# A graph convolution with residual and layer norm on one core: column bands of 1024, wider tiles, and transfers issued from two engines

## The chip, the cores and the metric

The kernel runs on one core of one Trainium2 chip. The metric is the device time of one execution in microseconds (us). Engines are called PE (TensorE, the matmul engine), DVE (VectorE), ACT (ScalarE), POOL (GpSimd) and SP (SyncE, which here only issues transfers). PEld is the weight load of PE, which runs beside its matmuls. A name with q behind it (SPq, ACTq) is the queue of transfers that the engine issues.

## The reference

```python
def reference(x, adj, L0_gnn_w):            # x 8192x128, adj 8192x8192, w 128x128, all float32
    A = adj + jnp.eye(8192)
    deg = jnp.sum(A, axis=1)
    d_isqrt = jax.lax.rsqrt(deg)
    A_hat = A * d_isqrt[:, None] * d_isqrt[None, :]
    y = x + jax.nn.elu(jnp.matmul(jnp.matmul(A_hat, x), w))
    return (y - mean(y)) / sqrt(var(y) + 1e-05)      # over the last axis
```

adj is 268 MB and dominates everything. Each of its elements is wanted twice: in a row sum, and in the product with x. Column j of the product needs the scale of row j of x, and so the whole of row j's sum, before it can be multiplied.

## The kernel before

adj is cut into 16 x 16 tiles of 512 rows by 512 columns (1 MB each). SBUF has `SLOTS` = 20 buffers for tiles (`tile0` to `tile19`), the last three of which are used at the end for the rows of the result.

A function `plan()` writes the order of the work out ahead of time. The columns are taken one after the other (`COLUMNS`: 14 single ones and the last two together). Before the products of column t can start, the rows of block t must have been read whole, because they give the scale of x's block t. So plan() alternates: it reads the rest of the rows of block t+1, and multiplies column t. Of a row block, some tiles to the right are kept in SBUF (`KEEP`, 7 or 8) until their column comes. The others are read for their row sum alone (kind `sum_only`) and read once more later (kind `again`). That makes 331 loads of 1 MB: 62 `keep`, 119 `stream` (below the diagonal, read once), 75 `sum_only` and 75 `again`. So 256 tiles are loaded for a product.

A tile for a product is laid out so that DVE's transpose of 32 x 32 blocks turns it: partition quadrant q (32 partitions) holds the columns 128q to 128q+127 of the tile, for 16 groups of 32 rows. Its load is 8 transfers of 128 KB, all issued by SP (L339): 4 quadrants times `PARTS` = 2 halves. Each contiguous piece in memory is 128 floats, 512 bytes. A `sum_only` tile is one transfer of 1 MB (L335) with pieces of 2 KB. SP waits before each load until the slot's last user is done.

Row sums are taken by ACT (L427, one activation with an accumulated sum for each group of 128 columns, or of 512 in a `sum_only` tile) for three tiles of five, and by POOL and DVE for the others: POOL adds halves (L389) and quarters (L393), and DVE reduces the rest (L574). POOL also adds 1 to the diagonal (L379). DVE turns the tile in place (L569). PE multiplies it: 4 matmuls of 512 columns in the source, which the trace shows as 8 MATMUL rows, since a float32 matmul is carried out in two (L502). DVE adds the product from PSUM to `hT` (L648, L646).

When a row block is read, DVE adds its partial sums (`row_base`, `row_sum`, L613), PE spreads them over the partitions (`p_deg`, L489), DVE copies the degree (L630), POOL raises it to -0.5 (L371), and DVE scales x (L637). SP loads x (L347) into a ring of 4.

The end of a row block of the result: PE multiplies `hT` by w (`p_out`, L475), ACT scales and takes relu and exp (L451 to L458), DVE makes the elu (L523), POOL adds x (L410), DVE takes the statistics (L532, L536), POOL the inverse deviation (L399, L403), DVE normalises (L543), and ACT stores (L440).

Each engine's order comes from the times that plan() works out from four costs:

```python
    LOAD, PRODUCT, SUMS, TURN = 2.91, 3.50, 4.2, 5.2
```

## Time and profile before

| | |
|---|---|
| median of 3 runs | 1421.13 us (1414.34 to 1422.74) |
| the profiled execution | 1416.74 us |
| its span, from the first to the last instruction | 1414.6 us |
| busy: PE, DVE, ACT, POOL | 961.3, 884.1, 642.2, 484.1 us |
| moved by DMA | 360.68 MB, mean 255 GB/s |
| mean granted clock of TensorE | 0.865 of full speed |

The busy times are those of single instructions, added up. A matmul's row is longer than its turn on the engine, because consecutive matmuls overlap. The last line is the share of its full clock that TensorE was granted.

### The profile page before, as it was taken

The page shows a single profiled execution, that of the slowest core. Times are in us where ns is not written, and L with a number is a line of the kernel's source. Part 1 is how long each engine was busy: PE and PEld are TensorE (multiplying, and loading weights), DVE is VectorE, ACT ScalarE, POOL GpSimd, SP SyncE. Part 2 cuts the span into 40 slices and gives each one's busy share as a digit, 9 for nine tenths or more (in the row PEclk, how much of TensorE's full clock was granted, in tenths as well). Part 3 has the DMA queues.
Part 4 walks back from the last instruction along what each step waited for, and adds up shares of the span by engine and source line. Part 5 has one row for each costly group of instructions (what it writes and reads, how often), then busy time and mean ns, then how long its engine had stood idle before and what let it go on. Part 6 is the DMA issues. An engine that isn't in the chain of part 4 may idle for free.

```text
span 1414.6 us, 12892 instructions
## 1 busy us (share of the span) xinstructions
PE 961.3 (68%) x2304; PEld 422.5 (30%) x2304; DVE 884.1 (62%) x979; ACT 642.2 (45%) x3713; POOL 484.1 (34%) x358
## 2 busy tenths in 40 slices
PE   0086097087095392956859495959687796899995
PEld 0032043033042141422324142424233342344542
DVE  0175275385364674746758574756657694988995
ACT  4576476456474563754626453333432202002333
POOL 3434434544434444233343333241312214101333
PEclk9999598599598696987979797979897898999998
DMA  9999999999999999999999999999999999999982
GB/s 305 248 259 328 299 246 316 283 240 317 249 244 313 255 304 257 240 287 257 271 237 282 238 271 238 247 243 249 248 238 238 253 240 242 235 205 242 270 200 66
DMA packets 624528, 360.68 MB, mean 255 GB/s; under 512 B 37056, under 2 KB 586048, under 8 KB 624448
## 3 DMA queue, kind: packets, MB, share of 16 engines
q1 hardware_dynamic: 606016, 351.48, 108.2%
q10 hardware_dynamic: 18432, 8.40, 2.6%
q14 instruction: 62, 0.51, 0.1%
q8 instruction: 18, 0.29, 0.1%
HBM read 355.53 MB, written 4.19 MB: 254 GB/s over the span
## 4 chain that ended last, share of the span: by engine, by line
issue 51%; POOL 28%; PE 11%; SPq 6%; DVE 3%; DMA 0%; POOLq 0%; ACT 0%; ACTq 0%; DVEq 0%
POOL halves L389 16%; PE p_prod L502 10%; POOL quarters L393 9%; SPq L339 5%; POOL tile L379 2%; DVE tile L569 2%; PE p_out L475 1%; SPq L335 1%; POOL d L371 1%; DVE hT L648 1%; DMA tile<-in_adj 0%; POOL tile L410 0%; DVE sums L622 0%; POOL rstd L403 0%; SPq L347 0%
## 5 line engine op out<-in xcount | busy, mean ns | idle before, releaser
L502 PE MATMUL p_prod<-tile,xs 128*128 128x512 f32 x2048 | 945.9, 622 | 90.4 <-DVE tile L569 83.7
L427 ACT ACTIVATE tile<-tile 128x128 f32<-128x128 f32 (+1 forms) x1800 | 586.1, 327 | 599.5 <-DMA tile<-in_adj 597.7
L569 DVE STREAM_TRANSPOSE tile<-tile 128x2048 f32<-128x2048 f32 x256 | 586.7, 2296 | 80.2 <-DMA tile<-in_adj 57.6
L502 PEld LDWEIGHTS p_prod<-tile,xs 128*128 128x128 f32 x2048 | 403.8, 200 | 610.0 <-issue 603.8
L389 POOL TENSOR_TENSOR halves<-tile 128x1024 f32<-128x1024 f32 x109 | 256.0, 2348 | 583.6 <-DMA tile<-in_adj 579.2
L427 ACT ACTIVATION_READ_ACCUMULATOR tile<-tile 128x1 f32 x1800 | 336.8, 187 | 0.0
L489 PE MATMUL p_deg<-rsum,same 128*32 128x4 f32 x128 | 4.4, 199 | 345.7 <-DVE rsum L613 340.3
L648 DVE TENSOR_TENSOR hT<-p_prod,hT 128x512 f32<-128x512 f32 x224 | 146.7, 660 | 16.8 <-PE p_prod L502 16.7
L393 POOL TENSOR_TENSOR quarters<-halves 128x512 f32<-128x512 f32 x109 | 137.9, 1265 | 8.6
L574 DVE TENSOR_REDUCE row_part<-quarters 128x16 f32<-128x512 f32 x30 | 20.4, 679 | 147.7 <-POOL quarters L393 147.7
L574 DVE TENSOR_REDUCE col_part<-quarters 128x16 f32<-128x512 f32 x50 | 33.8, 677 | 125.7 <-POOL quarters L393 125.5
L489 PEld LDWEIGHTS p_deg<-rsum,same 128*32 128x32 f32 x128 | 3.1, 131 | 357.3 <-DVE rsum L613 278.4
L574 DVE TENSOR_REDUCE far_part<-quarters 128x4 f32<-128x512 f32 x29 | 19.9, 686 | 116.1 <-POOL quarters L393 116.1
L451 ACT ACTIVATE tile<-p_out,d 128x128 f32<-128x128 f32 x64 | 18.2, 368 | 159.6 <-PE p_out L475 158.8
L379 POOL TENSOR_TENSOR tile<-tile,ident 128x128 f32<-128x128 f32 x64 | 27.2, 457 | 100.7 <-DMA tile<-in_adj 100.7
L371 POOL TENSOR_TENSOR d<-deg,power 128x4 f32<-128x4 f32 x16 | 16.3, 1017 | 104.9 <-DVE deg L630 104.9
L637 DVE TENSOR_SCALAR xs<-xs,d 128x128 f32<-128x128 f32 x64 | 26.2, 472 | 25.2 <-POOL d L371 25.2
L410 POOL TENSOR_TENSOR tile<-tile 128x512 f32<-128x512 f32 x16 | 20.3, 1269 | 55.2 <-DVE tile L523 53.1
L399 POOL TENSOR_SCALAR var_eps<-mv 128x4 f32<-128x4 f32 x16 | 7.8, 488 | 70.2 <-DVE mv L536 70.2
L543 DVE TENSOR_SCALAR tile<-tile,mv,rstd 128x128 f32<-128x128 f32 x64 | 19.4, 366 | 2.7 <-POOL rstd L403 2.7
L475 PEld LDWEIGHTS p_out<-w_sb,hT 128*128 128x128 f32 x128 | 16.7, 191 | 7.3 <-issue 7.2
L403 POOL TENSOR_TENSOR rstd<-var_eps,power 128x4 f32<-128x4 f32 x16 | 16.6, 1037 | 1.3
(28 smaller groups left out, 122.6 us busy)
## 6 DMA issues: line engine op xcount, KB each, us to landing
tile<-in_adj SPq DMA_DIRECT2D x2048, 128.0 KB, 4.0
tile<-in_adj SPq DMA_DIRECT2D x75, 1024.0 KB, 12.8
xs<-in_x SPq DMA_DIRECT2D x64, 64.0 KB, 3.6
tile<-in_x ACTq DMA_DIRECT2D x64, 64.0 KB, 5.0
out_rows<-tile ACTq DMA_DIRECT2D x64, 64.0 KB, 2.5
w_sb<-in_w SPq DMA_DIRECT2D x1, 64.0 KB, 1.9
```

The lines of the kernel that those rows point to most:

```text
L339: sp.dma_start(tiles[slot][quadrant(q), part], adj_v[s, t, q, :, part]).then_inc(loaded[slot], 16)
L371: nc.gpsimd.tensor_tensor(d[:, r], deg[:, :], power[:, :], ALU.pow).then_inc(d_ready, 1)
L379: nc.gpsimd.tensor_tensor(diag[:, b, :, 32 * b:32 * b + 32], diag[:, b, :, 32 * b:32 * b + 32], ident[:, :, :], ALU.add).then_inc(pool_ste ...
L389: nc.gpsimd.tensor_tensor(half, view[:, :, 0:c], view[:, :, c:2 * c], ALU.add).then_inc(pool_halved, 1)
L393: nc.gpsimd.tensor_tensor(quarter, half[:, :, 0:c // 2], half[:, :, c // 2:c], ALU.add)\
L427: ins = nc.scalar.activation(view[:, g], view[:, g], ACT.Copy, accum_out=sum_at(k)[:, g:g + 1])
L475: ins = nc.tensor.matmul(p_out[n % 2][:, b], hT[:, s, b], w_sb[:, :], start=True, stop=True)
L502: ins = nc.tensor.matmul(p_prod[nth % BANKS][:, :].rearrange("f (g i) -> f g i", g=G), xs[:, t % XRING, b], chunks[:, b], start=(t == cols ...
L569: nc.vector.transpose(tiles[slot][:, :, :], tiles[slot][:, :, :]).then_inc(tile_turned, 1)
L574: nc.vector.tensor_reduce(sum_at(arg), of_rows(how, quarters[:, pool_nth[arg] % 2]), AX.X, ALU.add)\
L637: ins = nc.vector.tensor_scalar(xs[:, r % XRING, b], xs[:, r % XRING, b], d[:, r, b:b + 1], None, ALU.mult)
L648: nc.vector.tensor_tensor(rows, product, rows, ALU.add).then_inc(product_added, 1)
```

## The change

adj is now cut into 8 column bands of 1024 columns (`WIDTHS`), and a tile is 256 rows by 1024 columns (still 1 MB; `rows_of(t)` = 256, `chunk(t)` = 256). There are 32 tiles in a band, 256 in all. In a partition quadrant the contiguous piece is now 256 floats, 1 KB.

Tiles are kept by one rule (`kept_units`): a tile on or above the diagonal is kept if at most `KEEP` = 14 are alive at every band from its rows' band to its own. What is not kept is read for its row sum as `natural`: 128 rows by 2048 columns, pieces of 8 KB (or two blocks of 128 rows by 1024 columns where an odd band is left, pieces of 4 KB). It is read again for the product.

A tile for a product is loaded by 4 transfers of 256 KB: quadrants 0 and 1 are issued by SP, quadrants 2 and 3 by ACT, each behind a wait for the slot. On ACT they stand in order between the row sums.

plan() is now a list scheduler. It plays through events (landed, summed, turned, multiplied), with at most 4 loads in flight, and each engine takes the first of its ready operations by rank. Its orders (`order["sp"]`, `["act"]`, `["pool"]`, `["dve"]`, `["pe"]`) are what the engines then execute, with semaphores. ACT or POOL takes a row sum by which of them would end it sooner. The bookkeeping for a degree is simpler: one table `part` for tiles and one `far` for natural loads, two reductions on DVE, and more small matmuls into `p_deg`. x is scaled by one DVE operation a band, and its ring has 3 places of twice the size. A product is 8 matmuls of 256 columns in the source. The rows of the result are loaded and stored by one transfer a step instead of four.

The core of the diff:

```diff
-NB = 16
-B = N // NB
-G = B // 32
-SLOTS = 20
-XRING = 4
-PARTS = 2
-KEEP = [7, 8, 8, 8, 8, 8, 8, 8, 8, 8, 7, 8, 8, 3, 8, 8]
+WIDTHS = [1024] * 8
+UNIT = 128 * 2048
+SLOTS = 20
+LATE = 3
+KEEP = 14
+XRING = 3
+SP_QUADRANTS = (0, 1)
+ACT_QUADRANTS = (2, 3)
...
+def kept_units():
+
+    spans = []
+    for t in range(BANDS):
+        for u in range(N // rows_of(t)):
+            r = band_of_row(u * rows_of(t))
+            if r <= t:
+                spans.append((t, -r, u))
+    alive, kept = [0] * BANDS, set()
+    for t, r, u in sorted(spans):
+        if all(alive[m] < KEEP for m in range(-r, t + 1)):
+            kept.add((t, u))
+            for m in range(-r, t + 1):
+                alive[m] += 1
+    return kept
...
+    def issue():
+
+        nonlocal dma, at_row, at_col, row_todo, col_todo
+        while in_flight[0] < 4:
+            coming = sum(1 for k in range(max(0, len(loads) - 24), len(loads)) if loads[k][0] != "natural"
+                         and loads[k][1] <= at_row - 1 and (loads[k][1], loads[k][2]) not in product_of)
+            usable = SLOTS - LATE if late() else SLOTS
+            slots = [s for s in free if s[1] < usable]
+            if not slots:
+                return
+            from_rows = row_todo and (not col_todo or coming >= 5)
...
             sp.dma_start(w_sb[:, :], w).then_inc(w_loaded, 16)
-            for k, (kind, s, t, slot) in enumerate(loads):
...
-                    for q, g in ((q, g) for pair in ((0, 2), (1, 3)) for g in range(0, G, G // PARTS) for q in pair):
-                        part = slice(g, g + G // PARTS)
-                        sp.dma_start(tiles[slot][quadrant(q), part], adj_v[s, t, q, :, part]).then_inc(loaded[slot], 16)
...
+                k, load = arg, loads[arg]
+                wait_slot_free(sp, k)
+                if load[0] == "natural":
+                    _, r, k0, nk, x0, wide = load
+                    row = STARTS[r] + 128 * k0
+                    source = adj[row:row + 128 * nk, x0:x0 + wide].rearrange("(k p) c -> p k c", p=128)
+                    sp.dma_start(tiles[slot_of[k]][:, 0:nk * wide].rearrange("p (k c) -> p k c", k=nk), source)\
+                      .then_inc(loaded[slot_of[k]], 16)
                 else:
...
+                    for q in SP_QUADRANTS:
+                        sp.dma_start(as_unit(tiles[slot_of[k]][quadrant(q)], t), quadrant_source(t, u, q))\
+                          .then_inc(loaded[slot_of[k]], 16)
...
         @block.scalar
         def _(act):
+            def issue(k):
+
+                _, t, u = loads[k]
+                wait_slot_free(act, k)
+                for q in ACT_QUADRANTS:
+                    act.dma_start(as_unit(tiles[slot_of[k]][quadrant(q)], t), quadrant_source(t, u, q))\
+                       .then_inc(loaded[slot_of[k]], 16)
+
+            def row_sums(k):
+
+                act.wait_ge(loaded[slot_of[k]], arrived[k])
+                view = as_summed(k, tiles[slot_of[k]][:, :])
                 for g in range(view.shape[1]):
                     ins = nc.scalar.activation(view[:, g], view[:, g], ACT.Copy, accum_out=sum_at(k)[:, g:g + 1])
                 ins.then_inc(act_summed, 1)
...
+                    chunks = tiles[slot_of[k]][:, :].rearrange("p (g b i) -> p b g i", b=nb, i=32)
+                    for b in range(nb):
+                        ins = nc.tensor.matmul(p_prod[n % BANKS][:, 0:rows_of(t)].rearrange("f (g i) -> f g i", i=32),
+                                               xs[:, t % XRING, b], chunks[:, b], start=b == 0, stop=b == nb - 1)
+                    ins.then_inc(product_out, 1)
```

## Rows read from the trace of the kernel before

**Rows 1.** The page: busy time of each engine with share, and packets by size.

```profile
PE 961.3 (68%) x2304; PEld 422.5 (30%) x2304; DVE 884.1 (62%) x979; ACT 642.2 (45%) x3713; POOL 484.1 (34%) x358
...
DMA packets 624528, 360.68 MB, mean 255 GB/s; under 512 B 37056, under 2 KB 586048, under 8 KB 624448
```

**Rows 2.** Waits: engine and line, whom it waited for, us in total, times, longest.

```profile
ACT tile L427 <- DMA tile<-in_adj: 597.7, 73, 51.0
POOL halves L389 <- DMA tile<-in_adj: 579.2, 71, 38.0
...
PE p_prod L502 <- DVE tile L569: 83.7, 28, 10.1
```

**Rows 3.** The page's DMA issues: count, KB each, median us from issue to landing.

```profile
tile<-in_adj SPq DMA_DIRECT2D x2048, 128.0 KB, 4.0
tile<-in_adj SPq DMA_DIRECT2D x75, 1024.0 KB, 12.8
```

**Rows 4.** Windows: length, busy us and count by engine, clock, DMA share, GB/s.

```profile
15.00:20.00 5.00, 0.00 (x0) 0.00 (x0) 0.00 (x0) 3.89 (x14) 0.75 (x1) 1.00 1.05 386
...
100.00:105.00 5.00, 5.00 (x13) 2.24 (x12) 3.21 (x4) 2.13 (x15) 4.54 (x3) 1.00 1.22 272
...
130.00:135.00 5.00, 1.58 (x4) 0.38 (x2) 1.22 (x3) 4.68 (x16) 0.00 (x0) 0.96 1.05 387
...
1350.00:1355.00 5.00, 5.00 (x13) 2.22 (x12) 4.97 (x15) 2.62 (x7) 0.80 (x2) 1.00 1.19 301
```

**Rows 5.** Line L339 from 100 to 119 us: its issues, duration in ns, min/median/max.

```profile
L339 SPq DMA_DIRECT2D tile<-in_adj x39: 448/451/481, 99.8 to 118.5; - x39
...
DMA to landing us min/median/max: 3.3/3.6/4.9
```

**Rows 6.** SP's timeline: start, length of the run of issues, line, count.

```profile
119.54 23.54 SPq L335 DMA_DIRECT2D tile<-in_adj  x12
...
1181.62 1.74 SPq L347 DMA_DIRECT2D xs<-in_x  x4
1183.40 178.23 SPq L339 DMA_DIRECT2D tile<-in_adj  x296
```

**Rows 7.** SP's own waits, the longest for a compute engine.

```profile
SPq L339 <- PE p_prod L502: 20.9, 23, 6.6
```

**Rows 8.** Windows of the product stage and of its last part (columns as in Rows 4).

```profile
200.00:300.00 100.00, 52.23 (x118) 22.12 (x117) 54.57 (x51) 58.95 (x346) 42.47 (x27) 0.76 1.11 282
...
1260.00:1330.00 70.00, 70.00 (x200) 33.98 (x199) 61.43 (x86) 17.51 (x42) 12.81 (x13) 1.00 1.22 249
```

**Rows 9.** The chain that ended last: start, length, what, with counts.

```profile
1379.82 0.89 PE p_out L475 x8
1380.71 6.87 PE p_prod L502 x16
...
1395.34 0.91 PE p_out L475 x8
```

**Rows 10.** DVE's and PE's timeline around the first degree.

```profile
70.15 0.18 DVE L613 TENSOR_TENSOR rsum<-rsum,base 128x16 f32<-128x16 f32 x1
...
74.66 2.07 PE L502 MATMUL p_prod<-tile,xs 128*128 128x512 f32 x2 [3.90 <-DVE xs L637]
```

**Rows 11.** Groups by line and shape: count, busy us, mean ns of one, idle before.

```profile
L569 DVE STREAM_TRANSPOSE tile<-tile 128x2048 f32<-128x2048 f32 x256 | 586.7, 2296 | 80.2 <-DMA tile<-in_adj 57.6 <-ACT tile L427 22.7
L427 ACT ACTIVATE tile<-tile 128x128 f32<-128x128 f32 x1616 | 472.8, 294 | 510.2 <-DMA tile<-in_adj 510.1
...
L389 POOL TENSOR_TENSOR halves<-tile 128x1024 f32<-128x1024 f32 x109 | 256.0, 2348 | 583.6 <-DMA tile<-in_adj 579.2 <-DVE far_part L574 0.7
L648 DVE TENSOR_TENSOR hT<-p_prod,hT 128x512 f32<-128x512 f32 x224 | 146.7, 660 | 16.8 <-PE p_prod L502 16.7
L393 POOL TENSOR_TENSOR quarters<-halves 128x512 f32<-128x512 f32 x109 | 137.9, 1265 | 8.6
L427 ACT ACTIVATE tile<-tile 128x512 f32<-128x512 f32 x184 | 113.3, 616 | 89.2 <-DMA tile<-in_adj 87.6
```

More of the change, by code:

```diff
@@ L186, in gcn_resnorm @@
-    last_read = {s: k for k, (kind, s, *_) in enumerate(loads) if kind != "again"}
-    x_after = {k - 3: s for s, k in last_read.items()}
-    pool_nth = {k: n + 1 for n, k in enumerate(k for kind, k in pool_steps if kind == "sum")}
-    act_nth = {k: n + 1 for n, k in enumerate(on_act)}
-    turned = [k for kind, k in vector_steps if kind == "turn"]
-    turn_nth = {k: n + 1 for n, k in enumerate(turned)}
-    load_of = {(s, t): k for k, (kind, s, t, _) in enumerate(loads) if kind != "sum_only"}
@@ L206, in gcn_resnorm, with nth_of @@
-    RING = G // CH
-    BANKS = 5
+    loads, slot_of, products, finals, order, _ = plan()
+    GROUPS = N // 32
+    BLOCKS = N // 128
+    PIECES = 4
+    NBMAX = max(WIDTHS) // 128
+    def nth_of(engine, kind):
+        return {arg: n + 1 for n, arg in enumerate(a for k, a in order[engine] if k == kind)}
+    act_nth, pool_nth = nth_of("act", "sum"), nth_of("pool", "sum")
+    turn_nth, add_nth, quarter_nth = nth_of("dve", "turn"), nth_of("dve", "add"), nth_of("dve", "quarters")
+    scale_nth, degree_nth = nth_of("dve", "scale"), nth_of("pe", "degree")
@@ new lines, in gcn_resnorm @@
+    load_of = {load[1:]: k for k, load in enumerate(loads) if load[0] != "natural"}
+    product_nth = {tu: n + 1 for n, tu in enumerate(products)}
+    band_products = {t: max(product_nth[v] for v in products if v[0] == t) for t in range(BANDS)}
+    arrived, counts, before, holder = [], [0] * SLOTS, [], {}
+    for k, load in enumerate(loads):
+        counts[slot_of[k]] += 16 if load[0] == "natural" else 16 * Q
+        arrived.append(counts[slot_of[k]])
+        before.append(holder.get(slot_of[k]))
+        holder[slot_of[k]] = k
@@ new lines, in gcn_resnorm @@
+    summed_rows = {r: [] for r in range(BANDS)}
+    natural_pieces = {k: 0 for k in range(BLOCKS)}
+    piece_at = {}
+    for k, load in enumerate(loads):
+        if load[0] == "natural":
+            _, r, k0, nk, _, _ = load
+            b0 = STARTS[r] // 128 + k0
+            piece_at[k] = (b0, natural_pieces[b0])
+            for b in range(b0, b0 + nk):
+                natural_pieces[b] += 1
+            summed_rows[r].append(k)
+        elif load[0] == "first":
+            summed_rows[band_of_row(load[2] * rows_of(load[1]))].append(k)
@@ L209, in gcn_resnorm @@
+    in_late = [k for k in range(len(loads)) if slot_of[k] >= SLOTS - LATE]
     with ExitStack() as ctx:
@@ L321, in _, with wait_slot_free @@
+        def wait_slot_free(engine, k):
+            old = before[k]
+            if old is None:
+                return
+            if loads[old][0] != "natural":
+                engine.wait_ge(product_out, product_nth[loads[old][1:]])
+            elif old in act_nth:
+                engine.wait_ge(act_summed, act_nth[old])
+            else:
+                engine.wait_ge(pool_summed, pool_nth[old])
         @block.sync
@@ L406, in add_residual @@
[L406 to L416 removed]
+                return steps
+            steps = 0
@@ L463, in _ @@
+            for kind, arg in order["act"]:
+                if kind == "issue":
+                    issue(arg)
+                elif kind == "sum":
+                    row_sums(arg)
+                elif kind == "residuals":
+                    first_residuals()
+                elif kind == "finish":
+                    finish(arg)
+                else:
+                    store(arg)
             for n in range(RING):
-                act.wait_ge(stored[n], 64 * len(range(n, NB, RING)))
+                act.wait_ge(stored[n], 16 * len(range(n, STEPS, RING)))
```

908 lines of the change are left out of this document (494 added, 414 removed).

## The prediction, made before the changed kernel ran

> **What bounds the kernel now.** I read the page's busy times first: no engine is above 68% [rows 1], so the time is set by waits, and the question is whose. The waits answer it: ACT and POOL, the first to touch a tile that lands, spend 597.7 and 579.2 us waiting for tile loads, while PE waits only 83.7 us for a turned tile in so many words [rows 2]. The loads are late nearly everywhere.
>
> Next I asked why a load takes as long as it does. Two kinds stand side by side. While the 2 KB pieces of `sum_only` tiles flow, the windows show 386 and 387 GB/s, or 1.049 MB / 387 = 2.71 us a tile. While the 512-byte pieces flow they show 272 [rows 4], 3.86 us a tile. The packet counts say that nearly all traffic is of the second kind: 586048 of 624528 packets are under 2 KB [rows 1]. In a stretch of such loads an issue on SP takes 448 to 481 ns, and 39 of them fill the 19 us [rows 5]: 8 x 0.48 = 3.85 us a tile. So one tile's issues alone take as long as the tile. The landing time points the same way. It stays at 3.6 to 4 us there, but goes to 12.8 us for the 1 MB transfers [rows 3, 5], whose queue is visibly full. Yet the DMA share is at its top (1.22) in the same windows, and one window with ACT's transfers beside SP's reaches only 301 GB/s [rows 4]. SP's issue rate and the small pieces are two limits that lie close together, and the change moves both.
>
> The last 150 us are another matter. From 1260 to 1330 us PE is busy throughout at full clock [rows 8], and the chain is PE alone: 6.87 us for 16 MATMULs of 512 columns (0.429 us each, 3.44 us a tile), then 0.89 us for `p_out` [rows 9]. Any speed-up of the loads ends where PE is the bound: 256 x 3.44 = 880 us, plus what comes before the first product and behind the last.
>
> **The change part by part.** *How many loads.* Working `kept_units` out for 8 bands of 4 row units keeps 64 tiles of the 144 on or above the diagonal. The other 80 tiles' worth is read twice. That is 256 quadrant loads (q) and 80 natural ones (n; 68 with 8 KB pieces, 12 with 4 KB) against 256 and 75 before. Five more megabytes cost 5 x 2.71 = 14 us, and are in the sums below.
>
> *Price of a quadrant load.* The trace has no 1 KB piece. It has two neighbours. At 272 GB/s a 512-byte packet takes one of the 16 engines 30.1 ns; at 387 GB/s a 2 KB one takes 84.7 ns. A straight line through both gives 11.9 ns and 0.0356 ns a byte, so 48.3 ns for 1 KB: 339 GB/s, 3.09 us a tile. The bounds are 2.71 us (the 2 KB rate) and 3.86 us (no gain). I take 3.09, since a price per packet plus one per byte is the plain reading of two points. The issue no longer binds: two transfers on SP are 0.96 us, two on ACT as much.
>
> The Trainium skill (page "DMA: Bandwidth & Descriptors", section "Issuing engines are not separate DMA queues") says that issuing from several engines saves only the time of the issuing sequencer, usually small beside the transfer. By that rule the split itself would be worth nothing and all of the gain would have to come from the larger pieces; here the issue time is not small, 3.85 of 3.86 us [rows 4, 5].
>
> *Price of a natural load.* 2.71 us is the nearest row. The same line gives 2.43 us at 8 KB, but one point beyond its ends is thin evidence. I take 2.60, with 2.43 and 2.71 as bounds.
>
> *The phases.* Let phase P(r) be the stretch that loads what is left of band r and the rows of band r+1. From the rule, the loads are: first rows 10q+22n; P0 36q+20n; P1 32q+16n; P2 32q+10n; P3 32q+8n; P4 32q+4n; P5 30q; P6 28q; P7 24q. Times at 3.09 and 2.60: 88, 163, 140, 125, 120, 109, 93, 87, 74 us, 999 in all. Each of the phases P0 to P7 has 32 products. Sixteen MATMULs of 256 columns stream as many columns as eight of 512. If the weight loads stay hidden, that is again 3.44 us a tile and 110 us a phase. That they stay hidden is to be seen in `p_out`: 8 MATMULs of 128 columns, each with its own weight load, take 0.89 us, 0.111 each [rows 9], half of what 256 columns need. The outer bound is 0.111 us more for each of the 2048 added MATMULs, 227 us; nothing speaks for it.
>
> So the loads set the pace through P3, and PE from P4 on. Loads to the end of P3: 88+163+140+125+120 = 636 us, and five loads of x (0.52 MB each, 1.9 us at 272 GB/s, taken at 2.1): 647.
>
> *The overhead of real life.* I checked this kind of sum on the kernel before. Up to 1183 us it has issued 75 `sum_only`, 219 quadrant tiles (256 less 296/8) and 16 blocks of x [rows 6]: 75 x 2.71 + 219 x 3.86 + 16 x 1.74 = 1076 us. It took 1183, a factor of 1.10, which is waits for slots [rows 7] and the changes between kinds. I apply it: 647 x 1.10 = 712. From the last row sum to the first product it took 4.5 us [rows 10], and the sum itself some 4; with the 3 us of the first transfer, band 4 starts at about 723.
>
> *The PE part.* P4, P5 and P6 are 330 us; with 3% for hiccups at three changes of band, 340. P7 has 32 products and 16 times `p_out`: 110 + 14 = 124. Behind the last product before lie 1414.6 - 1395.3 = 19 us of result work [rows 9], which has the same shapes. 723 + 340 + 124 + 19 = 1206 us of span, and 2.1 us around it as in the profiled execution: 1208. The profiled execution lay 4.4 us under the median of the runs, which is well inside my error, so I leave 1208.
>
> *The other engines.* DVE turns 256 tiles as before (2.296 us each, 588 us), adds 256 products of 256 columns at between 0.33 and 0.66 us instead of 240 at 0.66 [rows 11]: 84 to 169 us against 157. In a PE phase of 110 us it has 32 x (2.3 + 0.5) = 90 us of work. In the last part it was busy 61.43 of PE's 70 us [rows 8] with hardly less to do for each product, so in P7 it comes close to PE; a few us from that are in the spread. POOL's operations have the same shapes, 2.348 + 1.265 us. ACT's sum of a tile becomes 8 operations of 256 columns; between 294 ns for 128 and 616 for 512 [rows 11] lies 401, 3.2 us a tile instead of 4.7, and a natural load is one operation of about 1.9 us. With some 140 sums at 2.8 us that is 390 us, plus 512 issues at 0.45 us, 230 us: 620 of 1206. No engine beside PE becomes full.
>
> *What waits behind the new waits.* ACT now waits for a free slot, mostly for PE's product, with its row sums queued behind; DVE's turn and PE wait for those. I cost it at nothing beyond the factor 1.10, because with 14 kept tiles (the old plan had up to 13 alive, counted from its list) 6 slots remain. The cover is thin: if each of the 256 ACT issues held its sums up by 0.5 us uncovered, it would be 128 us. The bound below is nothing: an earlier sum cannot come from a wait.
>
> *TensorE's clock.* In the loads' stage the granted clock was 0.76 of full with PE busy 52% [rows 8], a mixture of its two levels, 1.2 and 2.4 GHz. At the lower one a tile takes twice 3.44, 6.9 us. In P0 PE has 110 us of work in 163, so some of that is to come again, covered by the loads; from P3 on PE is kept busy and I expect full clock.
>
> **The rivals.** *A: 1 KB pieces move like 2 KB pieces* (2.71 us). For it: 16 engines share a common ceiling, and 1 KB may already reach it. Against it: the step from 512 bytes to 2 KB is large. The loads are then first to fall behind PE through P2 only: (84 + 150 + 128 + 113 + 8) x 1.10 + 10 = 541, then P3 to P6 440 and 2% more, 990, P7 and tail 143, and 2: 1135 us.
>
> *B: 1 KB pieces move at the 512-byte rate* (3.86 us). For it: 272 GB/s came with a DMA share at its top, and ACT's transfers beside SP's gave no more than 301 [rows 4]; the pieces of a partition lie 32 rows, 1 MB, apart as before. (256 x 3.86 + 80 x 2.60 + 17) x 1.10 = 1334, and about 34 us from the last landing through sum, turn, product and tail: 1368 us. The skill's same page (section "Latency and other measured facts") reports that row pitches at large powers of two slow HBM transfers and that padding cures it; the pitch of 32 KB is the same here before and after, and the trace shows 387 GB/s at it with 2 KB pieces, so if that rule bites it is by way of this rival. That the change does not do what it says (the pieces are cut to 512 bytes again) gives the same time.
>
> *C, slower: ACT's in-order queue closes a loop.* ACT cannot issue its half of a later tile while it waits for the landing of the one that it must sum. If only one such pair of tiles is in flight, the loop is landing 4.9 us [rows 5] + sum 3.2 + two issues 0.9 = 9.0 us for two tiles, one summed by ACT and one by POOL: 4.5 us a tile. (256 x 4.5 + 80 x 2.60 + 17) x 1.10 + 34 = 1549 us. It decides from 4.05 us a tile on, a loop of 8.1 us: there (1037 + 208 + 17) x 1.10 + 34 = 1422, the time before. Against it: the plan puts up to four loads ahead of each sum, which cuts the loop to a quarter.
>
> **How the numbers follow.** My forecast, 1208 with its own spread of 1150 to 1300 (factor 1.03 to 1.15, DVE in P7, waits on ACT), has 0.56. A has 0.14, B 0.17, C 0.10; the last 0.03 lie within 1% of the time before, which is about what a measurement can tell from no change, by B and waits together. The range reaches from 1120, a little under A, to 1370, which takes in B at its reckoned price; C, the worse half of B and the luckier end of A stay outside, about 2 in 10. Faster by over 1%: 0.56 + 0.14 + 0.17 = 0.87. Within 1%: 0.03. Slower: 0.10.
>
> **What would show it.** The windows of the changed kernel should show about 339 GB/s while quadrant loads run and about 400 for natural ones. ACT's waits for tile loads should shrink in the second half and PE should be busy without a gap from about 720 us on at full clock; the chain should be PE's `p_prod` from there. A p_prod of 256 columns should come every 0.215 us. First products should start at about 100 us. The prediction is wrong if quadrant windows stay near 272 (B), if ACT's transfers are issued with long waits in front and ACT's sums stand behind them (C), or if DVE ends the chain in the last phase.

## The result, and the profile after

The changed kernel takes 1371.64 us (median of 3 runs, 1368.28 to 1373.26) against 1421.13. The ratio is 0.966, 95% interval 0.960 to 0.972: 3.4% faster where 15% was forecast. The time lies 1.6 us above the upper end of the stated range. In two later sessions the same kernel had medians of 1356.42 and 1356.96 us, with single runs from 1312.82 to 1392.02, beside 1419.60 and 1417.81 for the kernel before. It scatters far more than the old one, whose runs of all sessions lie between 1408.91 and 1430.98.

The page of the changed kernel, its lines in the order of those in [rows 1] and the page's rates; the last lines are its queues (q1 is SP's, q10 ACT's) and its issues:

```profile
PE 994.9 (73%) x4592; PEld 850.7 (62%) x4592; DVE 798.5 (58%) x850; ACT 474.3 (35%) x1577; POOL 438.0 (32%) x292
...
GB/s 389 385 338 350 271 256 244 236 236 323 313 243 235 237 270 308 238 237 241 250 297 299 284 283 310 345 312 260 168 292 272 197 248 289 289 254 256 288 80 62
DMA packets 317400, 365.94 MB, mean 267 GB/s; under 512 B 18704, under 2 KB 305552, under 8 KB 308624
...
q1 hardware_dynamic: 161168, 222.40, 59.0%
q10 hardware_dynamic: 156160, 142.64, 42.3%
...
tile<-in_adj SPq DMA_DIRECT2D x512, 256.0 KB, 9.0
tile<-in_adj ACTq DMA_DIRECT2D x512, 256.0 KB, 9.4
tile<-in_adj SPq DMA_DIRECT2D x80, 1024.0 KB, 16.9
```

The pieces are larger, as the change says: 317400 packets instead of 624528 for 5 MB more. ACT's and DVE's busy times fell as expected. But the mean rate went from 255 to 267 GB/s only. The row of rates shows where (a slice is 34 us): it begins at 389, lies near 240 in most slices from 170 to 650 us, with 313 and 323 around 340 us and 308 around 530 us, where natural loads pass, and reaches 345 only around 870.

Four stages of the changed kernel by windows (columns as in [rows 4]): two early column stages, the third, and a late one.

```profile
380.00:490.00 110.00, 78.58 (x294) 63.78 (x295) 64.74 (x52) 39.55 (x177) 43.41 (x25) 0.86 1.12 239
530.00:665.00 135.00, 96.58 (x385) 80.75 (x384) 75.14 (x63) 51.61 (x206) 52.90 (x31) 0.84 1.09 242
700.00:814.00 114.00, 95.30 (x397) 81.21 (x397) 79.25 (x64) 42.39 (x182) 45.78 (x27) 0.90 1.09 283
840.00:890.00 50.00, 50.00 (x233) 44.03 (x232) 41.03 (x36) 22.04 (x100) 21.85 (x12) 1.00 1.10 345
```

The first three and the last issue the same kind of transfer, and the DMA engines are counted as full in all four (1.09 to 1.12). In the last, with every compute engine busier than in the others, the transfers run at 345 GB/s, a little over the 339 of the prediction. In the first they run at 239. So the size of the pieces does not explain the low rate, and neither, by these four rows, does the load of the compute engines; something else differs between 400 and 860 us.

The queues tell what. The same view for 2 to 10 us at a time, q1 and q10 with packets, MB and share of the 16 engines' time. First 429 to 432 us, then 435 to 437, then 860 to 870:

```profile
q10 hardware_dynamic: 575, 0.56, 95.5%
q1 hardware_dynamic: 107, 0.10, 17.1%
...
q1 hardware_dynamic: 366, 0.35, 93.8%
q10 hardware_dynamic: 71, 0.07, 18.8%
...
q1 hardware_dynamic: 1799, 1.74, 55.3%
q10 hardware_dynamic: 1800, 1.73, 55.2%
```

In the slow stage the two queues take turns. In the 3 us ACT's moves 0.56 MB (187 GB/s) and SP's 0.10; then SP's moves 0.35 MB in 2 us (175 GB/s) and ACT's 0.07. Together they give 212 to 220 GB/s at each moment. In the fast stage each moves 174 GB/s all the time. SP's queue holds quadrants 0 and 1, ACT's 2 and 3, that is, partitions 0 to 63 and 64 to 127.

The queue that moves little is not empty. Counted from the issues and landings of the same trace, from 380 to 490 us SP has 3 to 9 transfers issued and not yet landed at every moment (6.2 in the mean) and ACT 2 to 8 (4.7 in the mean); from 840 to 890 us the means are 6.3 and 6.7.

### The profile page after: what moved, and what is told of

It is laid out like the page before. It is cut to its first block and busy times, and to the rows that moved or that the text cites. A ratio compares the mean times of both kernels' runs of the same rounds, so it can differ in the third digit from the quotient of the medians.

```text
span 1369.8 us, 13957 instructions
## 1 busy us (share of the span) xinstructions
PE 994.9 (73%) x4592; PEld 850.7 (62%) x4592; DVE 798.5 (58%) x850; ACT 474.3 (35%) x1577; POOL 438.0 (32%) x292
## 2 busy tenths in 40 slices
DMA packets 317400, 365.94 MB, mean 267 GB/s; under 512 B 18704, under 2 KB 305552, under 8 KB 308624
## 5 line engine op out<-in xcount | busy, mean ns | idle before, releaser
L733 PE MATMUL p_prod<-tile,xs 128*128 128x256 f32 x4096 | 970.5, 401 | 168.8 <-DVE tile L752 145.8
L733 PEld LDWEIGHTS p_prod<-tile,xs 128*128 128x128 f32 x4096 | 824.0, 203 | 308.1 <-issue 180.5
L631 ACT ACTIVATE tile<-tile 128x256 f32<-128x256 f32 (+2 forms) x732 | 412.1, 566 | 672.4 <-DMA tile<-in_adj 658.8
L583 POOL TENSOR_TENSOR halves<-tile 128x1024 f32<-128x1024 f32 x96 | 226.1, 2355 | 609.3 <-DMA tile<-in_adj 606.7
L756 DVE TENSOR_REDUCE part<-quarters 128x8 f32<-128x512 f32 x96 | 65.6, 683 | 243.6 <-POOL quarters L587 243.5
L794 DVE TENSOR_TENSOR hT<-p_prod,hT 128x256 f32<-128x256 f32 x224 | 89.4, 402 | 108.3 <-PE p_prod L733 107.3
L631 ACT ACTIVATION_READ_ACCUMULATOR tile<-tile 128x1 f32 x732 | 138.5, 189 | 0.0
L701 PEld LDWEIGHTS p_deg<-rsum,same 128*32 128x32 f32 x64 | 4.4, 132 | 189.5 <-issue 104.2
L573 POOL TENSOR_TENSOR tile<-tile,ident 128x256 f32<-128x256 f32 x32 | 23.4, 730 | 157.4 <-DMA tile<-in_adj 154.6
L598 POOL TENSOR_TENSOR d<-deg,half 128x16 f32<-128x16 f32 x8 | 23.3, 2912 | 43.5 <-DVE deg L779 43.5
L720 PE MATMUL p_out<-w_sb,hT 128*128 128x128 f32 x128 | 18.1, 287 | 6.6 <-DVE hT L794 6.6
```

The source lines that it names most:

```text
L573: nc.gpsimd.tensor_tensor(on_diagonal, on_diagonal, ident[:, q].unsqueeze(1).to_broadcast([128, g1 - g0, 32]), ALU.add)\
L583: nc.gpsimd.tensor_tensor(by_two, view[:, :, 0:c], view[:, :, c:2 * c], ALU.add).then_inc(pool_halved, 1)
L598: nc.gpsimd.tensor_tensor(d[:, arg, :, 0:nb], deg[:, :, 0:nb], half[:, :, 0:nb], ALU.pow).then_inc(d_ready, 1)
L631: ins = nc.scalar.activation(view[:, g], view[:, g], ACT.Copy, accum_out=sum_at(k)[:, g:g + 1])
L720: ins = nc.tensor.matmul(p_out[n % 2][:, b], hT[:, at:at + 128], w_sb[:, :], start=True, stop=True)
L733: ins = nc.tensor.matmul(p_prod[n % BANKS][:, 0:rows_of(t)].rearrange("f (g i) -> f g i", i=32), xs[:, t % XRING, b], chunks[:, b], start= ...
```

## The experiments

Those named "loads only" compute nothing of the reference: they load tiles of adj in stretches, drained one from the next, and their output is bytes of the loaded tiles. Their time as a whole means nothing; the rate in each stretch does. The others are whole kernels that compute the reference. Times are medians, beside the kernel before in the same session. The expectations name their theories by letters and say what each stands for where it first comes up. C in them is the compute engines' own traffic; the prediction's rival C comes back as L.

**m1, loads only: which stretch is slow.** Eleven stretches of 24 tiles.

```python
    ("band4 both", col(4, 8), "both"), ("band1 both", col(1, 8), "both"),   # SP 0,1; ACT 2,3
    ("band1 act behind", ...), ("band1 sp alone", ...), ("band1 and 3 in turn", ...),
    ("band1 quadrants crossed", ...),                                       # SP 0,2; ACT 1,3
    ("band4 act behind", ...), ("band1 two in flight", ...),
    ("pieces of 512 sp", ...), ("pieces of 512 both", ...), ("natural", ...)
```

> This kernel only loads tiles and computes nothing; its output is the first tiles' bytes. It runs 11 stretches of 24 tiles one after the other, each drained before the next: band 4, then band 1 with two quadrants on SP and two on ACT; band 1 with ACT held one landing behind SP; band 1 with all on SP; bands 1 and 3 in turn; quadrants crossed (0,2 and 1,3); band 4 with ACT behind; band 1 with two tiles in flight; 512-byte pieces on SP; the same on both; natural loads with 8 KB pieces. Theory Q (the rate falls from 347 to 240 GB/s when ACT's queue runs out of step with SP's): about 345 in all stretches in step and on SP alone, about 240 where ACT is behind, in both bands. Rival P (the rate is a matter of the place in adj): band 4 near 345 and band 1 near 240 whatever the queues do. Rival C (the engines' own traffic to SBUF slows the transfers): 340 or more everywhere, since nothing computes. 512-byte pieces: 270 on SP alone by the issue price, 300 on both if pieces limit. Natural: 400.

The windows inside the stretches, in that order (a kernel that only loads has POOL, clock, share and GB/s as columns):

```profile
20.00:60.00 40.00, 0.00 (x0) 1.00 1.10 346
100.00:140.00 40.00, 0.00 (x0) 1.00 1.10 347
180.00:220.00 40.00, 0.00 (x0) 1.00 1.10 346
260.00:340.00 80.00, 0.00 (x0) 1.00 1.13 223
370.00:420.00 50.00, 0.00 (x0) 1.00 1.10 347
450.00:530.00 80.00, 0.00 (x0) 1.00 1.13 229
570.00:610.00 40.00, 0.00 (x0) 1.00 1.11 345
640.00:720.00 80.00, 0.00 (x0) 1.00 1.12 267
740.00:830.00 90.00, 0.00 (x0) 1.00 1.22 239
850.00:920.00 70.00, 0.00 (x0) 1.00 1.22 290
940.00:990.00 50.00, 0.00 (x0) 1.00 1.01 423
```

Band 1 is as fast as band 4, so the place in adj (P) is out. ACT one landing behind costs nothing, so Q in its plain form fell too. Three stretches with 1 KB pieces were slow for reasons that none of the theories names: all on SP in the order 0, 1, 2, 3 (223), crossed (229), and two tiles in flight (267). In the first two, neighbouring transfers fill the same half of the partitions: 0 then 1 in one queue, or 0 beside 1 in two.

The third matters for the rest of this document. There each queue waits until the tile two before has landed whole, both then issue their halves within 0.1 us of each other, and no natural load is near. The queues take turns all the same, microsecond by microsecond (660 to 661 us, 661 to 662, 662 to 663):

```profile
q1 hardware_dynamic: 173, 0.18, 82.2%
q10 hardware_dynamic: 69, 0.07, 31.5%
...
q10 hardware_dynamic: 203, 0.20, 74.6%
q1 hardware_dynamic: 99, 0.09, 37.3%
...
q1 hardware_dynamic: 163, 0.17, 78.6%
q10 hardware_dynamic: 75, 0.07, 34.0%
```

So turns need no natural load and no late issue; few transfers in flight are enough. The price of the pieces comes out of m1 as well: 239 GB/s for the old form, 290 with the same 512 bytes on two queues, 347 with 1 KB on two, 423 with 8 KB (270, 300, 345 and 400 had been expected).

**e1, e2, e3: the same three questions put to the changed kernel.**

```diff
-SP_QUADRANTS = (0, 1)
-ACT_QUADRANTS = (2, 3)
+SP_QUADRANTS = (0, 1, 2, 3)    # e1
+ACT_QUADRANTS = ()             # e1
+SP_QUADRANTS = (0, 2)          # e2
+ACT_QUADRANTS = (1, 3)         # e2
```
```diff
                     for q in SP_QUADRANTS:      # e3; the same in ACT's issue(k)
+                        for h in (slice(0, 128), slice(128, 256)):
...
-                          .then_inc(loaded[slot_of[k]], 16)
+                              .then_inc(loaded[slot_of[k]], 16)
```

> The changed kernel with all four quadrants of a tile issued by SP, ACT issuing none. Theory Q (queues out of step cost the rate): the early column stages rise from 240 towards 340 GB/s and the kernel is faster by 60 us or more, near 1300. Rivals P and C: the rates stay, and the time is within 1% of 1370; if ACT's waits for slots had held its row sums up, a gain of 10 to 30 us.

> The changed kernel with quadrants 0 and 2 on SP and 1 and 3 on ACT. If which half of the partitions a queue writes matters, the early column stages change by more than 5% in rate; by theory Q, P and C alike nothing changes: 1370 within 1%.

> The changed kernel with each quadrant loaded in two transfers of 128 KB with pieces of 512 bytes, so 8 issues a tile, 4 on each queue. It takes the larger piece away and keeps the rest. If the size of the piece is what the change gained by, the rate of a pure quadrant stage at 840 to 900 us falls from 347 to 270 to 300 GB/s and the time rises to 1400 to 1450. If pieces do not matter once the issue is split, it stays within 1% of 1370.

Measured: e1 1530.97 us, e2 1462.67 (1.031 of the kernel before, interval 1.022 to 1.039), e3 1419.22 (0.997, 0.992 to 1.001), before 1418.57. With e1 theory Q is gone: one queue alone is slower by 160 us, not faster (its best run, 1477.69, is 86 us above the worst of the changed kernel's 13, 1392.02). e2 moves nothing but the pairing of quadrants and costs 6.6% against 1371.64; its expectation of "nothing changes" was a miss of all three theories. Where e2 loses is telling. Its early stage runs at 244 GB/s, where the changed kernel had 239; its late one, with PE busy throughout as in the changed kernel's 345 GB/s, runs at 265:

```profile
380.00:490.00 110.00, 73.45 (x290) 59.86 (x289) 63.16 (x52) 42.33 (x182) 39.77 (x22) 0.88 1.12 244
...
870.00:920.00 50.00, 50.00 (x233) 44.01 (x232) 37.03 (x32) 18.06 (x88) 18.16 (x10) 1.00 1.12 265
```

The pairing costs only where the changed kernel had its 345 GB/s; the early stages had lost it already. e3 has the large pieces cut in two and so twice the issues. Its late stage (840 to 900 us) falls to 292 GB/s, and the whole gain of the change is gone.

**m2, loads only: is it the queue or the half?** After m1 I formed theory H. The rival Q in its expectation is a new one: two queues are faster than one, whichever partitions they fill.

```python
    ("sp alone 0213", ...), ("sp alone, 0 and 1 only", ...), ("0 on sp, 1 on act", ...),
    ("0 on sp, 2 on act", ...), ("02 on sp, 31 on act", ...), ("six slots, in step", ...),
    ("six slots, act behind", ...), ("512 pieces, sp alone 0123", ...), ("512 pieces, sp 0213", ...)
```

> Loads only, as in the kernel with eleven stretches; nothing is computed. Nine stretches of 24 units of band 1. Theory H (a transfer to partitions 0 to 63 and one to 64 to 127 go at 347 GB/s side by side, and two to the same half share 223): quadrants 0 and 1 on SP alone about 223; 0 on SP beside 1 on ACT about 223 as well, although two queues are at work; 0 on SP beside 2 on ACT about 345; 02 on SP beside 31 on ACT about 345; six slots in step 300 or more; six slots with ACT behind about 230, because the two halves then take turns. Rival Q (two queues are faster than one, whichever partitions they fill): 0 beside 1 would be 345 like 0 beside 2. SP alone in the order 0213: H alone does not settle it: near 345 if transfers of both halves overlap in one queue, 223 if it works them off one by one. 512-byte pieces on SP: 223 in the order 0123, about 240 in the order 0213.

The windows in that order, the first five and the seventh:

```profile
20.00:100.00 80.00, 0.00 (x0) 1.00 1.13 236
120.00:170.00 50.00, 0.00 (x0) 1.00 1.13 203
180.00:230.00 50.00, 0.00 (x0) 1.00 1.13 206
250.00:270.00 20.00, 0.00 (x0) 1.00 1.10 346
300.00:370.00 70.00, 0.00 (x0) 1.00 1.12 263
...
500.00:530.00 30.00, 0.00 (x0) 1.00 1.10 346
```

The third and the fourth line decide it: two queues on one half move 206 GB/s, two queues on two halves 346. That much of H is shown, and the new Q refuted. (A quadrant is also a block of source columns, and no run parts the two; for SP alone in the order 0, 1, 2, 3 it made no difference whether neighbours lie 1 KB apart in a row of adj, 223 GB/s, or 2 KB, 224 in m3.) The Trainium skill (page "SBUF — State Buffer", section "Door 1: The DMA port swizzle") says of the ports between DMA and SBUF: of a partition's number it is the 64 that chooses the port of a pair, and the 32 changes nothing, so quadrants 0 and 1 reach only 8 of the 16 ports. By its figures that would be 217.6 GB/s, an estimate; the rows here that fill one half alone show 203 and 206, and no run here shows the ports themselves. Two of my numbers were misses: 02 beside 31 gave 263 and not 345, although its transfers meet in different halves, and six slots with ACT behind 346 and not 230 (after a slow start). Six slots in step gave 347. The 512-byte pieces gave 209 and 222.

**e4, e5, e6: order, pairing and slots in the kernel.**

```diff
-SP_QUADRANTS = (0, 1)
-ACT_QUADRANTS = (2, 3)
+SP_QUADRANTS = (0, 2, 1, 3)    # e4, ACT_QUADRANTS = ()
+SP_QUADRANTS = (0, 2)          # e5
+ACT_QUADRANTS = (3, 1)         # e5
-KEEP = 14
+KEEP = 11                      # e6
```

> The changed kernel with all quadrants on SP in the order 0, 2, 1, 3 instead of 0, 1, 2, 3. By theory H the order alone moves the rate if transfers overlap in one queue: faster than the one with 0123 (1531) by 100 us or more, 1300 to 1400. By rival Q the order is worth nothing: 1530 again.

> The changed kernel with quadrants 0 and 2 on SP and 3 and 1 on ACT. In step, the two queues always fill different halves; out of step, each queue alone has both halves in it. Theory H: at least as fast as 01 beside 23 (1372), perhaps 1300, and 60 us or more faster than 02 beside 13 (1463), from which it differs in the order of ACT's two transfers alone. Rival Q and P: the same as 02 beside 13, 1463.

> The changed kernel with KEEP 11 instead of 14: 343 loads instead of 336, and at least nine free slots instead of six at the end of each phase. If the two queues fall out of step because slots are short (theory S, an addition to H), the early column stages rise from 240 towards 300 GB/s and the time falls to 1280 to 1340 in spite of the added 7 MB. If slots are not the cause, the 7 loads cost about 20 us: 1390.

Measured: e4 1472.49 us (1435.32 to 1489.66), e5 1446.53 (1.019 of before, 1.011 to 1.026), e6 1432.42 (1391.43 to 1448.11), before 1417.77. In e4 the order alone is worth 58 us against e1, in e5 16 us against e2. Both point H's way, but the runs of each pair overlap (e4 up to 1489.66, e1 from 1477.69; e5 up to 1461.47, e2 from 1453.64), and neither reaches the number that I gave; H had expected e5 at 1372 or below. Theory S (slots are short) failed: the early stages, which it had rising from 240 towards 300 GB/s, ran at 224 and 247. The median rose by more than the 20 us of the added loads, though one run of four, 1391.43, lies where S's rival had it.

**e7, m3 and the kernel once more: do bursts of ACT part the queues?** In the slow stage ACT waits for a landing, starts a row sum and issues its halves of two tiles at once.

```diff
+                    if k in act_before:      # the last tile that ACT sums before it issues k
+                        j = act_before[k]
+                        sp.wait_ge(loaded[slot_of[j]], arrived[j])
                     for q in SP_QUADRANTS:
```

> The changed kernel with one more wait: before SP issues its half of a tile it waits for the landing that ACT's half of the same tile stands behind, so that both halves are issued together. Theory T (the queues take turns because ACT's issues come in bursts behind the landing of an earlier tile while SP runs ahead, and each turn fills one half of the partitions alone at about 217 GB/s): the early column stages rise from 237 to 300 GB/s or more although SP now waits more, and the time falls to 1200 to 1290. Rival L (ACT's loop alone sets the pace, 9.2 us for two tiles whatever SP does): 237 GB/s and 1370 stay. Rival W (an added wait only takes away transfers in flight): slower, 1400 to 1450.

> Loads only. ACT issues its halves two tiles at a time and waits before each pair for the landing of the tile three before. With SP free, theory T: about 240 GB/s, with each queue's share going up and down in turns; with the same waits on SP: 300 or more. With six slots the same as with 20, since SP is held a little more; with the tile five before and eight slots: SP free below 300, both waiting 345. Rival L: both forms of a pair are alike. 2 KB pieces: both queues 380, SP alone in order about 218 as with 1 KB, since the half sets it and not the piece.

> The changed kernel itself, once more, as the measure for the variants. All theories: 1372 if the state of its queues repeats; if the queues' step is a matter of chance, runs scatter as those with KEEP 11 did (1391 to 1448).

Measured: e7 1355.86 us (0.954 of before, 0.947 to 0.961), the changed kernel itself 1356.42, before 1419.60. All stretches of m3 with 1 KB pieces ran at 344 to 347 GB/s, whoever waited. Theory T fell in both: bursts do not part the queues, and a wait that brings the issues together does not join them (e7 ran at 255 and 267 GB/s from 380 to 490 and from 530 to 665 us, where T had 300 or more). W (an added wait costs) fell as well. L, that ACT's loop alone sets the pace, expected about this time and was still standing. 2 KB pieces gave 363 GB/s on both queues and 224 on SP in order, as expected.

What else differs between 400 and 860 us? The trace of the changed kernel has a candidate in the stretch where natural loads and tiles are mixed. The DMA queues from 110 to 117 us:

```profile
q1 hardware_dynamic: 311, 2.29, 88.9%
q10 hardware_dynamic: 294, 0.28, 13.9%
```

The queues get nearly the same number of packets, 311 and 294. But SP's are mostly of natural loads, up to 8 KB each, and ACT's are of 1 KB, so SP's queue moves 8 times as much. Equal counts are what one expects if the DMA engines take packets from the two queues in turn, and the Trainium skill says that they do (page "DMA: Bandwidth & Descriptors", section "Queues, rings and completion order"; its packet holds several pieces, the profile counts single ones). It cannot be the whole story: in the slow stage the counts were 575 and 107 with transfers of both queues waiting to land. While a natural load passes, ACT's halves hardly move; behind it the tile's other half is late, and so is everything that waits for the whole tile. Theory N is that this puts the queues out of step. Behind the 22 natural loads of the opening, 54 more stand among the tiles up to 814 us.

**m4, e8, e9: natural loads halved between the queues.**

```diff
-            if load[0] != "natural" and ACT_QUADRANTS:
-                offer("act", 0, "issue", k, 0.45 * len(ACT_QUADRANTS) + 0.05)
+            offer("act", 0, "issue", k, 0.5 if load[0] == "natural" else 0.45 * len(ACT_QUADRANTS) + 0.05)
...
+                if load[0] == "natural":
+                    natural_half(sp, k, slice(0, 64))
...
+                if loads[k][0] == "natural":
+                    natural_half(act, k, slice(64, 128))
+                    return
```

e9 is the same with the wait of e7.

> Loads, and beside the first stretch alone work for ACT, DVE and POOL that nobody uses. Stretches: tiles in step with engines busy; one natural load on SP before every two tiles; the same with the natural load halved between the queues (64 partitions each); four naturals and eight tiles, then 16 tiles alone; the same with eight slots; naturals of 2 KB pieces on SP; tiles in step with engines idle. Theory N (a natural load on one queue starves the other and leaves the two out of step): the halved form moves 360 GB/s or more, the form on SP alone 300 or less, and the tiles behind four naturals stay below 300 at least with eight slots. Rival C (the engines' work slows the loads): the first stretch is below 300 and the last at 345. Rival O (neither): tiles behind naturals return to 345 at once, the first stretch is at 345.

> The changed kernel with each natural load halved: partitions 0 to 63 on SP, 64 to 127 on ACT, at the place where ACT would issue a tile's half. Theory N: both queues carry the same bytes in the same order and stay in step; the rates from 140 to 700 us rise from 240 to 300 or more, the time falls to 1200 to 1290. Rival O (out of step for another reason, such as ACT's late issues): 237 stays in the stages without naturals, 1330 to 1370. Rival A (80 more issues in ACT's order hold up sums): 1370 to 1420.

> The same with the wait that makes SP issue its half where ACT does. By N as fast as the one without the wait or 10 to 40 us faster, since nothing is left that can part the queues; by O the same as without naturals halved, 1340 to 1370; by A slower, 1400.

Measured: e8 1345.35 us (0.947 of before, 0.939 to 0.954), e9 1343.63 (0.946, 0.938 to 0.954), before 1415.50. In loads alone N did badly, on all three of its numbers: with natural loads on SP between tiles m4 moved 324 GB/s (N: 300 or less), with halved ones 297 (N: 360 or more), and 16 tiles behind four natural loads ran at 348 at once, as rival O had it (N: below 300). The stretch beside busy ACT, DVE and POOL had 318 where the idle one had 346: a loss of 8%, not the 30% that C would need (ACT's issues also stood between its activations there, so this is not the engines' traffic alone). In the kernel the times of e8 and e9, 1345.35 and 1343.63, missed N's 1200 to 1290 and lie where O had them, 1330 to 1370. The rates speak for N and against O, which had 237 staying: 303 and 295 GB/s in e8's two stages, and more in e9. e9's windows, first the opening, then the two stages that had 239 and 242:

```profile
0.00:80.00 80.00, 0.00 (x0) 0.00 (x0) 2.04 (x2) 35.69 (x39) 1.69 (x12) 1.00 0.99 254
405.00:490.00 85.00, 71.24 (x299) 59.78 (x298) 65.86 (x53) 41.67 (x187) 45.23 (x26) 0.93 1.10 323
545.00:648.00 103.00, 77.95 (x325) 66.34 (x324) 74.29 (x62) 52.96 (x218) 53.04 (x31) 0.88 1.05 315
```

The column stages are at 323 and 315 GB/s. But the first natural loads, which have the queues to themselves and ran at 389 GB/s whole (381 over the same 80 us), run at 254 halved, and the first degree came at 146.7 us instead of 104.2. That is 42 us given back. (In e10, below, it came at 113.9; its expectation had the first product at 105 to 110.)

**e10, e11: halved only beside column loads.**

```diff
-            offer("act", 0, "issue", k, 0.5 if load[0] == "natural" else ...)
+            if not (load[0] == "natural" and load[1] == 0):
+                offer("act", 0, "issue", k, 0.5 if load[0] == "natural" else ...)
...
-                    natural_half(sp, k, slice(0, 64))
+                    natural_half(sp, k, slice(0, 128 if load[1] == 0 else 64))
```

e10 has the wait of e7, e11 has not.

> Natural loads of the first band's rows whole on SP, those of later bands halved between SP and ACT, and SP's half behind the same landing as ACT's. If natural loads in one queue are what makes the column stages slow (theory N), the first product comes at 105 to 110 us again, the stages from 140 to 700 us stay near 300 GB/s, and the time is the halved form's 1344 less about 40: 1295 to 1315. If the later start had merely moved work (rival M), 1340 to 1360.

> The same without the added wait on SP. Theory N: within 1% of the one with the wait, 1300 to 1320. Rival M: 1340 to 1360.

> The changed kernel itself beside them, for its scatter: a median of 1350 to 1370 with runs from 1315 to 1375, as seen before.

Measured, five rounds: e10 1296.83 us (1289.47 to 1313.34; 0.9135 of before, 0.909 to 0.918), e11 1307.81 (0.923, 0.919 to 0.928), the changed kernel 1356.96 (1312.82 to 1392.02), before 1417.81. N named 1295 to 1315 and M, that the later start had merely moved work, 1340 to 1360: N it is. e10's windows, and its queues from 380 to 460 us:

```profile
140.00:290.00 150.00, 105.20 (x435) 84.79 (x433) 86.23 (x73) 73.02 (x264) 52.47 (x29) 0.93 1.09 299
290.00:350.00 60.00, 14.62 (x107) 12.81 (x108) 20.97 (x19) 18.84 (x31) 22.13 (x15) 0.58 0.99 217
380.00:470.00 90.00, 73.52 (x329) 61.96 (x328) 73.74 (x60) 46.84 (x212) 52.12 (x31) 0.99 1.10 337
530.00:620.00 90.00, 67.33 (x285) 57.25 (x284) 76.40 (x62) 46.28 (x225) 53.05 (x31) 0.89 1.08 330
```

```profile
q10 hardware_dynamic: 12977, 13.40, 55.2%
q1 hardware_dynamic: 12973, 13.40, 54.2%
```

The two queues carry the same bytes, and the early stages run at 337 and 330 GB/s. The halved loads themselves are dear: where they pass, from 290 to 350 us, e10 moves 217 GB/s, and the changed kernel 316 in the like stretch (310 to 380 us). e10 is 8.6% faster than the kernel before. By the medians it is 4.4% faster than the changed one; best run against best run (1289.47 and 1312.82) it is 1.8%, and five of its six runs lie below all 13 of the changed kernel, the sixth at 1313.34. Its runs lie within 24 us, and those of the changed kernel beside it within 79.

## Why the prediction was wrong, point by point

**What bounds the kernel.** Right as far as it went. m1 confirms the two close limits: the old form alone moves 239 GB/s, the same pieces on two queues 290, larger ones on two queues 347. The old kernel's 272 [rows 4] is no property of 512-byte pieces. How much of what I read as issue time was two transfers meeting in one half, which the old order 0, 2, 0, 2 should mostly avoid, no run shows. The rule that the prediction quotes, by which issuing from two engines is worth no more than issue time, does not hold here: four issues of 0.48 us are 1.9 us of a tile that takes 4.7 us on SP alone (223 GB/s) and 3.0 on both (347).

**Price of a quadrant load.** 339 GB/s was forecast for 1 KB pieces, 345 to 347 measured wherever the queues kept step. Natural loads: 2.60 us forecast; 423 GB/s alone is 2.48 us. Both inside their bounds.

**The step that failed is "the overhead of real life".** The factor 1.10 was measured on a kernel with one queue and carried over to one with two. It had to cover the loads up to band 4, forecast at 712 us with it. SP asks for x's band 4, behind the last of those loads, at 814 us: 102 us more, and 1.26 instead of 1.10 over the bare sum of 647. What filled it was transfers at 239 and 242 GB/s instead of 345: at 345 the bytes of these two stages would take 171 us and not 245. It was not waits for slots, which take 27 of SP's 110 us in the first of the slow stages and 27 of 50 in the fast one. Even in the kernel before, SP's waits for slots up to 1183 us add up to only 60 of the 107 us that the factor stands for. I had counted the split over two queues as an issue-time matter only, and never asked which partitions each queue fills. That transfers to one half of the partitions share 206 GB/s where two halves get 346, and that natural loads in one of them cost the other its rate (with the later ones halved, e10 has 337 and 330 GB/s and asks for band 4 at 753 us instead of 814), was in none of my terms.

**The PE part.** This term was too small as well. Forecast 340 + 124 + 19 = 483 us; from 830 us to the end it was 540. Matmuls kept their price: 16 MATMULs of 256 columns took 3.46 us, 0.216 us each, against 0.215 forecast, so the weight loads are hidden. But the 3% for changes of band was too little. Two of them in the windows of the changed kernel:

```profile
955.00:975.00 20.00, 7.07 (x72) 5.90 (x72) 13.02 (x13) 8.44 (x41) 10.46 (x6) 0.67 0.88 183
...
1075.00:1092.00 17.00, 4.27 (x31) 3.36 (x30) 13.71 (x14) 6.61 (x32) 11.54 (x8) 0.68 0.86 190
```

PE is idle for 13 us of each, most of it (9.5 and 12.7 us) in waiting for the row sums of the next band's degree, and the granted clock is 0.67 and 0.68, part of it at the lower level of 1.2 GHz. From 830 to 1352 us PE is idle for 46 us of 522 where I had allowed 10, and busy for 476 where the sum had 454. The sum stated PE as the bound of these phases; at the changes it is the chain through the degree.

**The other engines, and the first product.** ACT 474 us and DVE 798 us busy, neither a bound; the first degree at 104 us where I said products at about 100. Right, near enough.

**The rivals.** B named 1368 us, 4 us from the measured time, and its sign in the profile (quadrant windows near 272 or less) is there in the early stages. That is luck. Its mechanism is refuted: 1 KB pieces move at 347, and e3, which really has 512-byte pieces, takes 1419. A right time from a wrong cause would have sent the next change to larger pieces; a gain lay in how natural loads are spread over the queues. C has its place in the trace: from 423 to 442 us ACT does issue two tiles at a time, 9 us apart, with 5 to 6 us of waiting for a landing in each loop, near the 9.0 us that I had worked out. But e10 keeps ACT's order of sums and issues in the column stages, issues two tiles every 6 us there, waits 2.4 to 3.0 us for a landing, and runs at 337 GB/s. So ACT's order alone does not make the loop long; with it fell theory L. A needed the 387 GB/s of the `sum_only` loads; 1 KB quadrant pieces stayed at 345 to 347 where nothing else was in their way, so it fell as well.

**What stays open.** Why the queues stay out of step in the kernel for 100 us after the last natural load, when loads alone recover at once (m4), is not settled. The kernel has a feedback that loads alone lack: the next issue waits for a whole tile that was summed, turned and multiplied. That this is what keeps the turns going is argued, not shown. A rival was not parted from N: too few transfers in flight. m1 has turns and 267 GB/s with two tiles in flight and no natural load, and ACT's queue held 4.7 transfers in the mean in the slow stage, 6.7 in the fast one and 7.6 in e10's from 380 to 470 us. Halving the natural loads may work by way of that. Nor does any run say why the queue with the smaller share gets so little while its transfers wait. Open as well are 02 beside 31 (263 GB/s), why natural loads halved between the queues are slow alone (254), and why KEEP 11 was slower.

## What to carry to other kernels

When transfers fill less than all 128 partitions, look at which half (0 to 63, 64 to 127) each fills, and keep transfers to both halves in flight together. Transfers to one half alone shared 203 to 206 GB/s here, whether one queue issued them or two. Keep more than two tiles in flight; with two the rate was 267 GB/s where it was 346. Where loads with large pieces and loads with small ones share two queues, try to give both queues the same bytes: it was worth 4.4% by the medians here, although it made the large loads slower. A factor for overhead measured on one design says little about another that shares its transfers out in a new way. When a DMA share is full at a low rate, read the queues one by one over a few microseconds.

## What the runs showed of the hardware that was not expected

- One queue with quadrants in the order 0, 1, 2, 3 moves 223 GB/s at 1 KB and 224 at 2 KB; in the order 0, 2, 1, 3 it is 236, and two queues, one on each half, move 346 and 363.
- Two queues with packets of up to 8 KB and of 1 KB got 311 and 294 packets in 7 us, and so 2.29 and 0.28 MB.
- Two queues with 1 KB pieces, one on each half, move 346 GB/s with many tiles in flight and 267 with two; with two they take turns of about 1 us (173 and 69 packets, then 99 and 203).
- Natural loads alone were faster in the opening as one transfer of 128 partitions on one queue (381 GB/s over the first 80 us of the changed kernel) than as two of 64 on two queues (254 in e9, where SP's issues also waited for landings; 252 in e8, where they did not).
- The share of DMA time is 1.10 at 347 GB/s and 1.13 at 203: it does not tell a fast stream from a slow one.
